# One-column transposes for the last key: ct_fill in a fused perceiver layer

## The chip, the cores and the metric

The kernel runs on one core of a Trainium2 chip. The metric is the device time of one execution in microseconds (us). Engines are called as the profile calls them: PE is TensorE's matmul side and PEld its weight loads, DVE is VectorE, ACT is ScalarE, POOL is GpSimd, SP is SyncE. Everything is fp32 unless it says otherwise.

## The reference

One layer over x (32 batches of 32 tokens, 512 wide) and a context of 257 keys per batch (384 wide). Cut to what matters here:

```python
def _L0_xattn_ref(x, context, g_x, b_x, g_c, b_c, Wq, Wk, Wv, Wo):
    xn = layer_norm(x, g_x, b_x)
    cn = layer_norm(context, g_c, b_c)          # context: (32, 257, 384)
    q = (xn @ Wq) ...; k = (cn @ Wk) ...; v = (cn @ Wv) ...      # 16 heads of 64
    sim = jnp.einsum('bhid,bhjd->bhij', q, k) * scale            # j runs over 257 keys
    attn = jax.nn.softmax(sim, axis=-1)
    out = jnp.einsum('bhij,bhjd->bhid', attn, v)
    return out.transpose(0, 2, 1, 3).reshape(B, N, INNER) @ Wo

x = x + _L0_xattn_ref(_layernorm(x), ctx_768, ...)   # cross attention, 257 keys
x = x + _L0_attn_ref(_layernorm(x), ...)             # self attention, 32 tokens
x = x + _L0_ffn_ref(_layernorm(x), ...)              # 8 experts, the best 2 per token
```

## The kernel before

The work is split into 8 groups of 4 batches (128 tokens). The function `body(g, do_a, do_b, nxt)` writes one round of every engine's instructions in a fixed order: `do_a` is the cross attention of group g, `do_b` the self attention and the routing of group g - 1, and `nxt` prepares group g + 1. Rounds 1 to 6 are a hardware loop; the others are written out. After the last round come the experts (lines 770 to 860). Each engine works through its own list in order and waits on semaphores; what PE does next is therefore exactly what stands next in `body`.

The keys need care: 257 is 128 + 128 + 1. The table `PART = [P, P, 65]` says how many partitions each of the three pieces of a batch's normalised context `ctx` takes. The last key stands on partition 0 of its piece (and copies of it on 32 and 64, which a later split product uses). `ct_fill` turns one 128-column slice c of one batch's context: three transposes on PE, each with `ctx` as the weights and the identity as what streams, write into the bank `TP` at the column offsets `KOFF = [0, 128, 256]`. The last one increments `tp_full`. ACT's `ct_out` (line 1129) then copies `TP[:, 0:KEYS]`, 257 columns, into `cnT` and frees the bank with `tp_free`. `scores` (line 1755) multiplies with `cnT`; the columns of `TP` from 257 on are read by nobody.

There are 3 calls of `ct_fill` per batch, 96 in all. By what stands behind them on PE (in `body`, round by round):

- `scores`, fp32 weights: the calls at b == 0, 3 in each of 8 rounds, 24 in all
- `av`, `av_high` or `av_low`, fp16 weights: the calls at b == 1 and b == 2, 48 in all, and two of the three calls for the next group's first batch, 14 in all; together 62
- another transpose with fp32 weights, `pt_fill` (line 1779) or `setup_fill`: 7 + 1
- another `ct_fill`, which waits for `tp_free`: 2, at the very start

[...]

Of the kernel before, what the change touches and what calls it, by code (L numbers as in the profile page):

```python
# [26 lines left out]
P = 128  # L27
# [17 lines left out]
GB = P // TOK  # L45
# [6 lines left out]
PART = [P, P, 65]  # L52
KOFF = [0, P, 2 * P]
# [41 lines left out]
def perceiver_layer(nc, x, ctx_768, g_x, b_x, g_c, b_c, Wq, Wk, Wv, Wo, W_qkv, W_o,  # L95
                    gate_w, gate_b, w1, b1, w2, b2, ln_g, ln_b, out):
    with ExitStack() as stack:
        def sb(name, shape, dt=F32):
            return stack.enter_context(nc.sbuf_tensor(name, shape, dt))
# [28 lines left out]
        ctx = arena[:, 0:4608].rearrange("p (s k c) -> p s k c", s=GB, k=3)  # L128
# [41 lines left out]
        ident = sb("ident", [P, P])  # L170
# [119 lines left out]
        TP, M, BK = bank[4], [bank[5], bank[6]], bank[7]  # L290
# [1387 lines left out]
        def _(pe):  # L1678
# [80 lines left out]
            def ct_fill(n, bt, b, c):  # L1759
                pe.wait_ge(tp_free, n)  # L1760
                if c == 0:
                    pe.wait_ge(cn_done, bt + 1)
                for k in range(3):
                    last = nc.tensor.transpose(TP[:, KOFF[k]:KOFF[k] + PART[k]], ctx[0:PART[k], b % GB, k, c * P:(c + 1) * P],  # L1764
                                               ident[0:PART[k], 0:PART[k]])
                last.then_inc(tp_full, 1)

            def pt_fill(g, b, k):
# [136 lines left out]
            def body(g, do_a, do_b, nxt):  # L1905
# [4 lines left out]
                if isinstance(g, int) and g == 0:  # L1910
                    pe.wait_ge(wk_in, 16)
                    for n in range(8):
                        setup_fill(n)
                    for c in range(KC):
                        ct_fill(1 + c, 0, 0, c)
                    pe.wait_ge(qkv_in, 16)
                    pe.wait_ge(wos_in, 16)
                    for n in range(8, 16):
                        setup_fill(n)
# [12 lines left out]
                for b in range(GB + 1):  # L1932
                    if do_a and nxt and b == GB:
                        ct_fill(tp(g, ("ct", GB, 0)), GB * g + GB, GB, 0)
                    for h in range(HG):
                        if do_a and b < GB:
                            scores(g, b, h)
                        if do_b and b == 1 and h == 0:
                            v_fill(g - 1)
                        if do_a and b == 0 and h < 3:  # L1940
                            ct_fill(tp(g, ("ct", 1, h)), GB * g + 1, 1, h)
                        if isinstance(g, int) and g == 0 and b == 1 and h in (0, 2):
                            keep_short(16 if h == 0 else 40, BK)
                        if do_a and b >= 1 and h < 3:
                            pt_fill(g, b - 1, h)
# [106 lines left out]
```

## Time and profile before

| | |
|---|---|
| median of 3 runs | 1328.2 us (1325.65 to 1328.8) |
| the profiled execution: its time, its span | 1326.96 us, 1325.3 us |
| mean granted clock of PE | 0.993 |
| PE busy, share of the span | 1277.7 us, 96% |
| PEld, DVE, ACT busy | 72%, 73%, 73% |
| one steady group (round) | 90.2 us |
| the 96 transposes of 65 partitions: records' sum | 21.3 us |

Read it so: a PE record lasts longer than the time that PE gives to it, because records of one engine overlap (they are pipelined). What an instruction costs PE is the distance from its start to the start of the next, here called its slot. The groups' rounds fill the span from about 120 to 740 us with a period of 90.2 us.

### The profile page before, as it was taken

The page shows a single profiled execution, that of the slowest core. Times are in us where ns is not written, and L with a number is a line of the kernel's source. Part 1 is how long each engine was busy: PE and PEld are TensorE (multiplying, and loading weights), DVE is VectorE, ACT ScalarE, POOL GpSimd, SP SyncE. Part 2 cuts the span into 40 slices and gives each one's busy share as a digit, 9 for nine tenths or more (in the row PEclk, how much of TensorE's full clock was granted, in tenths as well). Part 3 has the DMA queues.
Part 4 walks back from the last instruction along what each step waited for, and adds up shares of the span by engine and source line. Part 5 has one row for each costly group of instructions (what it writes and reads, how often), then busy time and mean ns, then how long its engine had stood idle before and what let it go on. Part 6 is the DMA issues. An engine that isn't in the chain of part 4 may idle for free.

```text
span 1325.3 us, 34868 instructions
## 1 busy us (share of the span) xinstructions
PE 1277.7 (96%) x11476; PEld 952.9 (72%) x11477; DVE 971.1 (73%) x2140; ACT 963.9 (73%) x1741; POOL 219.1 (17%) x270
## 2 busy tenths in 40 slices
PE   7999999999999999999999789999999999999997
PEld 7768768677697696786876666777777777777773
DVE  5775878877877878788766757776767676767677
ACT  3577776776777777776877537787888888888784
POOL 1001002012030120030210213121212121111112
PEclk9999999999999999999999889999999999999999
DMA  9527246154363372552732895546262626710104
GB/s 365 191 101 255 90 159 223 63 209 169 99 252 122 110 250 87 182 198 68 255 146 90 317 344 166 222 168 201 95 214 80 228 79 229 277 32 16 32 9 135
DMA packets 69838, 216.36 MB, mean 163 GB/s; under 512 B 5582, under 2 KB 5820, under 8 KB 64652
## 3 DMA queue, kind: packets, MB, share of 16 engines
q1 hardware_dynamic: 63568, 201.71, 42.0%
q0 software_dynamic: 6192, 13.98, 5.1%
q8 instruction: 31, 0.51, 0.1%
q14 instruction: 19, 0.16, 0.0%
q10 hardware_dynamic: 28, 0.01, 0.0%
HBM read 169.46 MB, written 46.22 MB: 163 GB/s over the span
## 4 chain that ended last, share of the span: by engine, by line
PE 67%; DMA 9%; issue 8%; DVE 7%; ACT 4%; POOL 3%; SPq 1%; DVEq 0%; POOLq 0%; ACTq 0%
PE bank L799 7%; PE bank L1755 7%; PE bank L787 6%; PE bank L789 6%; PE bank L801 6%; PE bank L800 6%; PE bank L788 6%; DMA w_halves<-arena 4%; DMA w_halves<-moe_w 3%; PE bank L1804 3%; PE bank L1789 3%; PE bank L1821 3%; PE bank L1792 2%; PE bank L1764 2%; PE bank L1889 2%
## 5 line engine op out<-in xcount | busy, mean ns | idle before, releaser
L787 PE MATMUL bank<-arena,moe_w 128*128 128x128 f16 x1472 | 256.2, 220 | 0.9 <-DVE arena L630 0.9
L789 PE MATMUL bank<-arena,moe_w 128*128 128x128 f16 x1472 | 256.4, 220 | 0.0
L788 PE MATMUL bank<-arena,moe_w 128*128 128x128 f16 x1472 | 255.6, 219 | 0.0
L1755 PE MATMUL bank<-moe_w 128*128 128x257 f32 x768 | 188.6, 383 | 0.0
L787 PEld LDWEIGHTS bank<-arena,moe_w 128*128 (+1 forms) x1472 | 143.8, 98 | 14.9 <-DVE arena L630 1.2
L788 PEld LDWEIGHTS bank<-arena,moe_w 128*128 (+1 forms) x1472 | 144.1, 98 | 10.3
L1755 PEld LDWEIGHTS bank<-moe_w 128*128 128x128 f32 x768 | 137.9, 190 | 17.7
L789 PEld LDWEIGHTS bank<-arena,moe_w 128*128 (+1 forms) x1472 | 143.8, 98 | 1.5 <-issue 0.2
L490 ACT ACTIVATE arena<-bank,now_act 128x128 f32<-128x128 f32 x368 | 136.8, 449 | 7.9 <-PE bank L789 4.5
L506 ACT ACTIVATE wosT<-moe_w,now_act 128x1024 f16 (+1 forms) x90 | 98.5, 1143 | 37.7 <-PE bank L801 37.7
L1147 ACT ACTIVATE moe_w<-bank,cols,ugain 128x512 f32<-128x512 f32 x96 | 74.4, 776 | 59.7 <-PE bank L1805 58.7
L438 POOL DMA_INDIRECT acc_rows<-arena,job_idx x22 | 52.1, 2368 | 396.3 <-DVE arena L671 396.3
L1377 DVE TENSOR_TENSOR moe_w<-bank,moe_w 128x512 f16<-128x512 f32 (+1 forms) x96 | 65.4, 689 | 48.1 <-ACT moe_w L1161 45.8
L647 DVE SCALAR_TENSOR_TENSOR arena<-moe_w,now_v,wosT 128x1024 f16<-128x1024 f16 (+1 forms) x45 | 57.8, 1285 | 52.5 <-ACT wosT L506 50.3
L647 DVE SCALAR_TENSOR_TENSOR kqT<-moe_w,now_v,y 128x1024 f16<-128x1024 f16 (+1 forms) x45 | 57.8, 1285 | 51.3 <-ACT y L506 51.0
L1009 POOL TENSOR_TENSOR crstd<-cmv,half 128x3 f32<-128x3 f32 x32 | 28.7, 898 | 396.1 <-DVE cmv L1334 396.1
L1161 ACT CAST moe_w<-bank 128x512 f16<-128x512 f32 (+1 forms) x96 | 54.3, 585 | 47.2 <-PE bank L1779 46.9
L506 ACT ACTIVATE y<-moe_w,now_act 128x1024 f16 (+1 forms) x45 | 51.7, 1149 | 43.5 <-PE bank L801 43.5
L1789 PE MATMUL bank<-moe_w 128*128 128x512 f16 x192 | 73.0, 380 | 3.7 <-DVE moe_w L1377 1.8
L1792 PE MATMUL bank<-moe_w,arena 128*128 128x512 f16 x192 | 72.6, 378 | 0.0
L1140 ACT ACTIVATE moe_w<-bank,negm 128x257 f32<-128x257 f32 x128 | 59.0, 467 | 15.9 <-DVE negm L1357 15.3
L638 DVE SCALAR_TENSOR_TENSOR arena<-arena,now_h 128x512 f16<-128x512 f32 x92 | 68.7, 746 | 1.6 <-ACT arena L498 1.6
(296 smaller groups left out, 3099.3 us busy)
## 6 DMA issues: line engine op xcount, KB each, us to landing
moe_w<-in_L_ffn_w_dram SPq DMA_DIRECT2D x46, 1024.0 KB, 6.4
moe_w<-w_halves SPq DMA_DIRECT2D x8, 4096.0 KB
moe_w<-in_L_ffn_w_dram SPq DMA_DIRECT2D x8, 4096.0 KB
w_halves<-moe_w SPq DMA_DIRECT2D x48, 512.0 KB, 4.2
arena<-in_ctx_dram SPq DMA_DIRECT2D x32, 384.0 KB
arena<-in_L_ffn_w_dram SPq DMA_DIRECT2D x10, 1024.0 KB, 4.9
blocks<-in_L_ffn_w_dram SPq DMA_DIRECT2D x8, 1024.0 KB, 4.8
w_halves<-arena SPq DMA_DIRECT2D x8, 512.0 KB
```

Of the source, the lines that this page charges most:

```text
L490: last = nc.scalar.activation(h_sb[:, fb % 2, c * P:(c + 1) * P], bank[fb][:, c * P:(c + 1) * P], ACT.Gelu, bias=now_act[:, 4 + 4 * fb + c ...
L506: nc.scalar.activation(v_place(0, j, fb, i), moe_flat[:, bass.ds(slot * 16384 + 8192 + fb * 2048 + i * 1024, 1024)], ACT.Identity, scale=n ...
L647: nc.vector.scalar_tensor_tensor(out=v_place(1, j, fb, i), in0=moe_flat[:, bass.ds(slot * 16384 + 8192 + fb * 2048 + i * 1024, 1024)], sca ...
L787: nc.tensor.matmul(into, high, xT_low[turn][:, k, :], start=(k == 0), stop=False)
L788: nc.tensor.matmul(into, high, xT_high[turn][:, k, :], start=False, stop=False)
L789: last = nc.tensor.matmul(into, low, xT_high[turn][:, k, :], start=False, stop=(k == KD - 1))
L799: nc.tensor.matmul(Y[:, :], hT_low[:, fb % 2, c, :], high, start=(fb == 0 and c == 0), stop=False)
L800: nc.tensor.matmul(Y[:, :], hT_high[:, fb % 2, c, :], high, start=False, stop=False)
L801: last = nc.tensor.matmul(Y[:, :], hT_high[:, fb % 2, c, :], low, start=False, stop=(fb == 3 and c == 3))
L1755: last = nc.tensor.matmul(bank[h][:, 0:KEYS], qkT[:, c, b, h * P:(h + 1) * P], cnT[:, b % 2, c, :], start=(c == 0), stop=(c == KC - 1))
L1789: nc.tensor.matmul(ps[:, :], n_high[:, b % 2, k, columns], pT_high[:, k, :], start=(k == 0), stop=False)
L1792: nc.tensor.matmul(ps[:, :], n_low[:, b, k, columns], pT_high[:, k, :], start=False, stop=False)
```

## The change

In `ct_fill` the third transpose of each call takes 1 partition and 1 column (`n_rows = 1`), where it took 65 and 65. It writes column 256 of `TP` alone. The first two transposes, the semaphores and all other engines' instructions are as they were; `PART` itself is unchanged, so the normalisation and the split products still handle 65 partitions.

```diff
@@ ct_fill
                 for k in range(3):
-                    last = nc.tensor.transpose(TP[:, KOFF[k]:KOFF[k] + PART[k]], ctx[0:PART[k], b % GB, k, c * P:(c + 1) * P],
-                                               ident[0:PART[k], 0:PART[k]])
+                    n_rows = P if k < 2 else 1
+                    last = nc.tensor.transpose(TP[:, KOFF[k]:KOFF[k] + n_rows], ctx[0:n_rows, b % GB, k, c * P:(c + 1) * P],
+                                               ident[0:n_rows, 0:n_rows])
                 last.then_inc(tp_full, 1)
```

[...]

PE's list at b == 1, where a call of `ct_fill` stands between two fp16 products of `av` (a row is: line, operation, output<-inputs, output's partitions x columns, how many in a row), before:

```order
L1805 MATMUL bank<-moe_w 128x512
L1764 MATMUL bank<-ident,arena 128x128 x2
L1764 MATMUL bank<-ident,arena 128x65
L1789 MATMUL bank<-moe_w 128x512
L1792 MATMUL bank<-moe_w,arena 128x512
```

and now (the line numbers are one higher):

```order
L1806 MATMUL bank<-moe_w 128x512
L1765 MATMUL bank<-ident,arena 128x128 x2
L1765 MATMUL bank<-ident,arena 128x1
L1790 MATMUL bank<-moe_w 128x512
L1793 MATMUL bank<-moe_w,arena 128x512
```

Nothing moved; one row is narrower. PE's list at b == 0, where the calls stand between `scores` (line 1755), before:

```order
L1755 MATMUL bank<-moe_w 128x257 x3
L1764 MATMUL bank<-ident,arena 128x128 x2
L1764 MATMUL bank<-ident,arena 128x65
L1755 MATMUL bank<-moe_w 128x257 x3
L1764 MATMUL bank<-ident,arena 128x128 x2
```

and now:

```order
L1755 MATMUL bank<-moe_w 128x257 x3
L1765 MATMUL bank<-ident,arena 128x128 x2
L1765 MATMUL bank<-ident,arena 128x1
L1755 MATMUL bank<-moe_w 128x257 x3
L1765 MATMUL bank<-ident,arena 128x128 x2
```

Again only the third transpose differs, and the order is the same on every engine.

## Rows read from the trace of the kernel before

**Rows 1.** The page: busy time, granted clock, the chain's shares.
```profile
PE 1277.7 (96%) x11476; PEld 952.9 (72%) x11477; DVE 971.1 (73%) x2140; ACT 963.9 (73%) x1741; POOL 219.1 (17%) x270
...
PEclk9999999999999999999999889999999999999999
...
PE 67%; DMA 9%; issue 8%; DVE 7%; ACT 4%; POOL 3%; SPq 1%; DVEq 0%; POOLq 0%; ACTq 0%
```
**Rows 2.** Windows: stretch, length, PE, PEld, DVE, ACT, POOL busy, clock, DMA share.
```profile
290.00:380.20 90.20, 88.66 (x682) 67.78 (x682) 71.94 (x191) 66.04 (x117) 14.51 (x18) 1.00 0.46 160
...
790.00:1325.00 535.00, 522.69 (x5570) 370.51 (x5566) 375.87 (x560) 421.38 (x780) 99.62 (x104) 0.99 0.42 139
```
**Rows 3.** Groups by line and shape: weights, what streams, count, busy us, mean ns.
```profile
L1764 PE MATMUL bank<-ident,arena 128*128 128x128 f32 x192 | 39.7, 288 | 4.8 <-ACT moe_w L1129 2.1 <-DVE moe_w L1377 2.0
...
L1889 PE MATMUL bank<-wosT,kqT 128*128 128x512 f32 x64 | 28.9, 593 | 0.5 <-ACT kqT L1165 0.5
L1764 PE MATMUL bank<-ident,arena 65*128 65x65 f32 x96 | 21.3, 222 | 0.0
...
L1994 PE MATMUL bank<-ident,arena 8*128 8x8 f32 x16 | 1.1, 201 | 0.0
...
L1870 PE MATMUL bank<-arena,kqT 128*32 128x128 f32 x32 | 1.1, 276 | 0.0
```
**Rows 4.** Timeline of PE: one call of ct_fill; start us, duration us, what.
```profile
158.71 0.38 PE L1805 MATMUL bank<-moe_w 65*128 65x512 f16 x1
158.93 0.44 PE L1764 MATMUL bank<-ident,arena 128*128 128x128 f32 x3
159.21 0.38 PE L1789 MATMUL bank<-moe_w 128*128 128x512 f16 x1
```
**Rows 5.** Timeline of PE: from 128x128 tiles to 128x64 tiles.
```profile
180.69 3.60 PE L1889 MATMUL bank<-wosT,kqT 128*128 128x512 f32 x8
184.22 5.73 PE L1821 MATMUL bank<-moe_w 128*64 128x128 f32 x96
```
**Rows 6.** Timeline of PE: into 128x32 tiles and out of them.
```profile
145.15 0.38 PE L1805 MATMUL bank<-moe_w 65*128 65x512 f16 x1
145.47 1.08 PE L1870 MATMUL bank<-arena,kqT 128*32 128x128 f32 x32
146.48 0.50 PE L1764 MATMUL bank<-ident,arena 128*128 128x128 f32 x3
```
**Rows 7.** Timeline of PE and PEld: into 32x128 tiles and out, last round.
```profile
767.71 1.45 PE L1889 MATMUL bank<-wosT,kqT 128*128 128x512 f32 x3
769.09 0.39 PE L1974 MATMUL bank<-ident,most_rows 16*128 16x16 f32 x2
...
769.56 1.13 PE L1994 MATMUL bank<-ident,arena 8*128 8x8 f32 x16
770.62 0.61 PE L1687 MATMUL bank<-ident 128*128 128x256 f16 x4
...
770.62 0.44 PEld L1687 LDWEIGHTS bank<-ident 128*128 128x128 f16 x5
```
**Rows 8.** Timeline of PE: scores behind line 1739, then behind ct_fill.
```profile
37.09 1.57 PE L1755 MATMUL bank<-moe_w 128*128 128x257 f32 x6
...
38.78 1.52 PE L1755 MATMUL bank<-moe_w 128*128 128x257 f32 x6
```
**Rows 9.** Timeline of DVE, ACT and PEld: third ct_fill of a steady round.
```profile
310.29 0.55 DVE L1308 TENSOR_SCALAR arena<-x_all,mv,rstd 128x512 f32 x1 [0.68 <-POOL rstd L1004]
...
311.21 0.48 ACT L1140 ACTIVATE moe_w<-bank,negm 128x257 f32<-128x257 f32 x1 [0.96 <-DVE negm L1357]
...
312.70 0.31 PEld L1764 LDWEIGHTS bank<-ident,arena 128*128 128x128 f32 x3 [0.46 <-ACT moe_w L1129]
```
**Rows 10.** Waits of PE in the steady round: us, times, longest.
```profile
PE bank L1764 <- DVE moe_w L1377: 0.3, 2, 0.2
PE bank L1833 <- ACT moe_w L1134: 0.3, 1, 0.3
```

## Prediction

> **What bounds the kernel now.** I read the page first. PE is busy for 96% of the span and holds 67% of the chain, while DVE and ACT stand at 73% [rows 1]. [...] The waits say the same: PE's two largest in the round are 0.3 us each, and all five rows of that answer together make 1.3 us [rows 10]. So during the rounds PE's own list sets the pace, and whatever a call of `ct_fill` costs more or less is paid almost in full, 96 times. The experts behind (535 us, [rows 2]) start when the rounds are over and hold no `ct_fill`; they shift as a block.
>
> **What the third transpose costs today.** Its record lasts 222 ns [rows 3], but that is not its price. In one call the three transposes start at 158.93 and `av`'s first product at 159.21 [rows 4]: 0.28 us for three slots. The two wide ones take 0.109 us each (three records last 0.44 us together, and the last of them 0.222, so two slots are 0.22), which leaves 0.06 us for the third. The whole that could be saved is thus 96 x 0.06 = 5.8 us, not the 21.3 us of the records' sum.
>
> **What it would cost if nothing but the width changed.** [...] The nearest row is line 1994: 16 transposes of 8 columns start 62 ns apart (1.13 us for 16, the last lasting 0.20, so 15 slots in 0.93) [rows 3, 7]. With an fp32 operation behind it the slot of a one-column transpose therefore stays at 0.06. Behind it stands fp16 in 62 calls; there the bounds are 0 and 0.06 us saved, and I would take half, 0.03 us, 2 us in all. [...]
>
> [...] The trace has passages between tiles, and each shows the same gap:
> - Into 128x64: eight records of line 1889 last 3.60 us, the last 0.593 [rows 3, 5], so their slots are 3.01 / 7 = 0.43, and the last starts at 183.70. Line 1821 starts at 184.22, 0.52 later: 0.09 more than a slot.
> - Into 128x32: line 1805 has 0.32 us before line 1870 [rows 6], and 0.22 us before line 1764, which has its own tile [rows 4]: 0.10 more.
> [...]
> - Out of 128x32: the last record of line 1870 starts at 145.47 + 1.08 - 0.276 = 146.27, line 1764 at 146.48 [rows 3, 6]: 0.20 for 128 fp32 columns that take 0.11, so again 0.09 to 0.10.
> [...]
>
> [...]
>
> The second part of the price is the weights. After a passage the load is no longer hidden: three transposes of line 1764 last 0.50 us behind line 1870 and 0.44 where their weights came early [rows 4, 6], 0.06 for fp32 transpose weights; `scores` takes 1.57 us behind line 1739's 64x128 tile and 1.52 behind `ct_fill` [rows 8], 0.05 more. For fp16 weights (line 1687, 1789) I take 0.01; no row above separates it, and 0 to 0.03 are its bounds.
>
> **One call, from the second transpose's start to the next operation's start.** Before: 0.11 + 0.06 = 0.17. After: 0.11, drain 0.09, the third's own weights 0.06, its one column practically 0, drain 0.10: 0.36. That is +0.19, and with the next operation's exposed weights +0.20 before fp16 and +0.24 before fp32. The lower bound takes the own load as hidden and the way out as line 1994 showed it: 0.09 + (0.13 - 0.06) = 0.16. The upper bound is +0.26 everywhere.
>
> **The sum.** 62 calls x 0.20 = 12.4; 24 + 8 calls before fp32 x 0.24 = 7.7; the two at the start, where PE waits for ACT anyway and only the bank's filling comes later (0.09 + 0.06), 0.3. Together 20.4 us.
>
> **What waits give back.** Where PE stands still today for something that does not depend on the calls just before, the delay fills the hole. One such place is clear. In each round the third call at b == 0 waits (0.46 us by the loader's row, 312.70) for ACT's `ct_out`, which is queued behind an exp that waited 0.96 us for DVE, which had waited for POOL's rstd [rows 9]. None of these comes after the first two calls. Line 1755 ahead lets PE start every 0.22 us; the wide first transpose came about 0.22 late and with its weights exposed (0.06): 0.28 us a round, 2.2 us in 8. The calls behind `av` wait a little for ACT too; I give them another 0.8 us. That makes 3 us absorbed. Bounds: nothing, and all 1.3 us of a round's waits [rows 10], 10 us in 8 rounds. Most of these waits follow PE's own `pt_fill` through ACT and DVE and would only move, so I stay near the lower. ACT gets `tp_full` 0.15 us later in each call, which ACT, busy 66 of 90 us, can take; and if DVE or ACT fell behind through it the next to be late would be `scores`' row maximum.
>
> 20.4 - 3.0 = +17.4 us. The profiled execution took 1326.96 us (span 1325.3), so 1344.4; the median shown is 1.2 us above it. I predict **1345 us**.
>
> **Rivals.**
> - *The forecast*: two drains a call, 1345 us (1338 to 1351 as its own range). [...] Chance 0.78.
> - [...] Chance 0.04, of which 0.03 lie within 0.3%. [...]
> - *Half price*: the way in or the way out overlaps with the transposes around it, so a call costs 0.10 to 0.12: 96 x 0.11 - 2 = +8.5, 1336 us. For it: no row shows a single instruction in a foreign tile; each passage above has several on either side. Chance 0.10.
> - *More than the sum*: `tp_full`'s delay also lengthens the chain through ACT and DVE, or a lone instruction pays 0.26 with nothing absorbed: +25, 1353 us. Against it: ACT and DVE have 18 us to spare per round [rows 2]. Chance 0.08.
>
> **How the numbers follow.** A measurement of this kernel can tell about 0.3%, 4 us, from no change. Faster by more 0.01; within 0.03; slower 0.96. The range of 8 in 10 leaves out the not-slower case, half of the half-price case, and the far end above: 1337 to 1351.
>
> **What would show it.** In the profile after, line 1765's record of one partition should start 0.20 us after the second transpose (0.11 before), and the operation behind it 0.15 to 0.17 us later (0.06 before). Its weight load should start with it and not ahead, and the next load should start only with the next operation. The steady round should last 92.2 to 92.6 us where it lasted 90.2, the experts' stretch should stay at 535 us, and the third call at b == 0 should no longer wait. The clock should stay at 1.00 in the rounds. I am wrong if that narrow record starts 0.11 after the second transpose, or if the round grows by less than 1.5 us with the gaps as forecast: then waits took more than I allowed.

## The result

The changed kernel takes 1341.2 us (median of 6 runs, 1336.8 to 1343.3), the kernel before 1327.4 us in the same comparison (6 runs): ratio 1.0099, interval 1.0084 to 1.0114. It is slower by 13.8 us or 1.0%. Forecast were 1345 us, a range of 1337 to 1351, and slower.

The page of the changed kernel, to be read against [rows 1]: PE is busier (1297.5 us against 1277.7), its weight loads take 8 us more, and the other engines are as they were. PE's share of the chain is 83% where it was 67%; a second profile of the same kernel has 73%, so nothing below rests on it.

```profile
PE 1297.5 (97%) x11476; PEld 961.1 (72%) x11477; DVE 971.7 (72%) x2140; ACT 963.6 (72%) x1741; POOL 218.0 (16%) x270
...
PE 83%; DVE 5%; ACT 5%; DMA 3%; issue 2%; POOL 1%; DVEq 0%; POOLq 0%; ACTq 0%; SPq 0%
```

Its groups by line and shape, to be read against [rows 3]: the narrow transpose's record is 4 ns shorter (218 against 222). By that row nothing has changed; the loss stands only in the distances between starts, and in the loader's idle time, 16.1 us or 0.17 us for each of the 96, with nothing that it waited for.

```profile
L1765 PE MATMUL bank<-ident,arena 1*128 1x1 f32 x96 | 21.0, 218 | 0.0
...
L1765 PEld LDWEIGHTS bank<-ident,arena 1*128 1x128 f32 x96 | 12.9, 134 | 16.1 <-issue 16.1
```

Timeline of PE and PEld in the changed kernel, one call before an fp16 product (start us, duration us, what), to be read against [rows 4]:

```profile
162.94 0.53 PE L1765 MATMUL bank<-ident,arena 128*128 128x128 f32 x3
...
163.25 0.14 PEld L1765 LDWEIGHTS bank<-ident,arena 1*128 1x128 f32 x1 [0.17 <-issue]
163.40 0.10 PEld L1790 LDWEIGHTS bank<-moe_w 128*128 128x128 f16 x1
163.41 0.39 PE L1790 MATMUL bank<-moe_w 128*128 128x512 f16 x1
```

From the first transpose to the product it is 0.47 us, where it was 0.28: unrounded, 0.18 more. Three records last 0.53, the last 0.218, so the third starts at 163.25, 0.20 us after the second (two wide slots of 0.11 would have put it at 163.16), and the product comes 0.15 after it (0.06 before). Each of the two weight loads starts only when its operation does (163.25, and 163.40 for the product at 163.41). These are the two gaps that the forecast calls drains.

What the traces show is the weights' partitions x columns and the starts. No view prints an array tile, and none shows the array being emptied; where the prediction and the titles of [rows 5, 6, 7] speak of tiles and drains, they are my reading of the gaps. In [rows 7] the weights are 16*128 and 8*128. Below, a passage is a change of the weights' partitions x columns after which PE's next start is 0.07 to 0.10 us later than its slots account for. Not every change is one: from line 1805's 65*128 weights to line 1764's 128*128 it is 0.22 us [rows 4], as between two products of 128*128 (141.96 to 142.18, lines 1789 and 1792 of the kernel before).

The windows, round by round (stretch, length, busy times, clock, DMA). First a steady round of the changed kernel, then rounds 0 to 3 of a second profile of it (the run e10 below), in all four of which the clock was 1.00:

```profile
389.26:480.74 91.48, 90.56 (x682) 68.36 (x683) 71.92 (x191) 65.93 (x117) 14.27 (x18) 1.00 0.45 157
```
```profile
11.53:110.02 98.49, 93.38 (x747) 73.72 (x746) 64.52 (x173) 58.94 (x114) 7.29 (x9) 1.00 0.59 212
110.02:203.52 93.50, 90.50 (x684) 68.29 (x682) 69.81 (x176) 68.99 (x120) 9.86 (x13) 1.00 0.44 152
203.52:295.18 91.66, 90.60 (x682) 68.36 (x683) 72.01 (x191) 65.89 (x117) 14.42 (x18) 1.00 0.44 157
295.18:386.75 91.57, 90.60 (x683) 68.37 (x683) 71.97 (x191) 65.93 (x117) 14.37 (x18) 1.00 0.45 158
```

and the same rounds of the kernel before, cut at the same places in its program:

```profile
11.59:108.18 96.59, 91.15 (x747) 73.25 (x746) 64.14 (x172) 58.69 (x114) 7.29 (x9) 1.00 0.59 216
108.18:199.79 91.61, 88.57 (x683) 67.70 (x682) 69.78 (x176) 68.92 (x120) 9.85 (x13) 1.00 0.46 157
199.79:290.05 90.26, 88.66 (x682) 67.78 (x683) 71.97 (x191) 65.83 (x117) 14.41 (x18) 1.00 0.45 159
290.05:380.24 90.19, 88.66 (x682) 67.78 (x683) 71.93 (x191) 66.04 (x117) 14.51 (x18) 1.00 0.46 160
```

So rounds 0 and 1 grew by 1.9 us each and the steady ones by 1.4. The forecast had 2.0 to 2.4 for a steady round. Twelve calls cost clearly more than the round grew, and the experiments look for the difference. One more sign of the forecast did not hold in the first profile: its clock was not at 1.00 in all the rounds, but 0.83 at 120 to 130 us (see e10).

### The profile page after: what moved, and what is told of

Its sections match the earlier page's. It is cut to its first block, busy times and chain, and to the rows that moved or that the text cites. A ratio compares the mean times of both kernels' runs of the same rounds, so it can differ in the third digit from the quotient of the medians.

```text
span 1340.3 us, 34868 instructions
## 1 busy us (share of the span) xinstructions
PE 1297.5 (97%) x11476; PEld 961.1 (72%) x11477; DVE 971.7 (72%) x2140; ACT 963.6 (72%) x1741; POOL 218.0 (16%) x270
## 4 chain that ended last, share of the span: by engine, by line
PE 83%; DVE 5%; ACT 5%; DMA 3%; issue 2%; POOL 1%; DVEq 0%; POOLq 0%; ACTq 0%; SPq 0%
PE bank L1755 9%; PE bank L799 6%; PE bank L787 6%; PE bank L789 6%; PE bank L801 6%; PE bank L800 6%; PE bank L788 6%; PE bank L1718 4%; PE bank L1834 4%; PE bank L1790 3%; PE bank L1739 3%; PE bank L1805 3%; PE bank L1822 3%; PE bank L1765 3%; PE bank L1793 3%
```

## The experiments

All times are medians. e2, e3, e4 and e7 ran on one chip, beside a kernel before at 1326.4 us; e5, e6, e8 and e10 on another, beside one at 1327.5. "Call" is the distance from a call's first transpose to the operation behind it, at b == 0; it is 0.28 us in the kernel before and 0.46 in the changed one. All of them replace the loop in `ct_fill`; the diffs are against the changed kernel, written with this helper:

```python
def turn(k, rows):
    return nc.tensor.transpose(TP[:, KOFF[k]:KOFF[k] + rows], ctx[0:rows, b % GB, k, c * P:(c + 1) * P],
                               ident[0:rows, 0:rows])
```

**e2: 33 partitions instead of 1.**

```diff
-                    last = turn(k, P if k < 2 else 1)
+                    last = turn(k, P if k < 2 else 33)
```

> [...] Theory (the passage between tiles costs, whatever the tile): the third starts 0.20 us after the second and the next operation about 0.17 us after it (0.15 with one column, and 33 fp32 columns stream 0.03 longer), so about 2 us above the changed kernel, 1343 us. [...]

Measured: 1343.0 us, ratio 1.0123 (1.0104 to 1.0142). Timeline of PE, one call:

```profile
407.25 0.56 PE L1764 MATMUL bank<-ident,arena 128*128 128x128 f32 x3
407.74 1.57 PE L1755 MATMUL bank<-moe_w 128*128 128x257 f32 x6
```

The call takes 0.49 us, 0.03 more than with one column. The third starts at 407.56, 0.20 us after the second, as in the changed kernel, and `scores` 0.18 after it, where it is 0.15 with one column. So it is no matter of one partition: 33 have the same two gaps, but for the 32 further columns, and the slots of 0.11 and 0.06 did not come back. The weights of line 1739, 64*128, have the gap on the way in too: 124.91 to 125.12 in the kernel before, 0.10 over line 1855's slot of 0.11. Beside weights of 128*128, those of 1, 8, 16, 33 and 64 partitions have a gap and those of 65 have none (e3); by what rule, no run shows.

**e4: the one-partition transpose twice in a row.**

```diff
                 turn(0, P)
                 turn(1, P)
+                turn(2, 1)
                 last = turn(2, 1)
```

> [...] Theory (price per passage): the second one starts 0.06 us after the first, its weights in the same tile, so 0.06 us a call more, 1345 to 1347 us. Rival (price per narrow instruction): again 0.20 and 0.15, so 0.2 to 0.3 us a call more, 1362 to 1368 us.

Measured: 1345.5 us, ratio 1.0143 (1.0127 to 1.0158). The call:

```profile
411.60 0.59 PE L1764 MATMUL bank<-ident,arena 128*128 128x128 f32 x4
412.12 1.57 PE L1755 MATMUL bank<-moe_w 128*128 128x257 f32 x6
```

0.52 us, 0.06 more than with one. Inside the call the narrow ones start at 411.91 and 412.00:

```profile
412.00 0.20 PE L1764 MATMUL bank<-ident,arena 1*128 1x1 f32 x1
412.12 0.48 PE L1755 MATMUL bank<-moe_w 128*128 128x257 f32 x1
```

So the second starts 0.085 us after the first, not the 0.06 of the expectation, and the next operation 0.125 after the second, where it is 0.147 after a single one. The two together make the 0.06. The price of a passage is not paid again; it belongs to the change from wide weights to narrow ones and back, and not to the narrow instruction. One column more costs, net, the 0.06 us that line 1994's eight did.

**e5: four passages instead of two.**

```diff
                 turn(0, P)
+                turn(2, 1)
                 turn(1, P)
                 last = turn(2, 1)
```

> Order of a call: wide, one-partition, wide, one-partition (the first one-partition transpose is a repeat of the last). Four passages where the changed kernel has two, and as many narrow transposes as in the kernel that did it twice in a row. Theory (each passage 0.09 us plus the weights that it exposes): 0.09 + 0.15 + 0.06 = 0.30 us a call over the changed kernel, and as the waits of the round are used up already nearly all of it shows: the steady round takes 94.8 to 95.1 us, the run 1366 to 1370 us. Rival (the price was that of a narrow transpose or of the end of a call): 0.06 us a call as with twice in a row, 1346 us.

Measured: 1367.0 us, ratio 1.0298 (1.0281 to 1.0316). The call, and the steady round:

```profile
423.33 0.83 PE L1764 MATMUL bank<-ident,arena 128*128 128x128 f32 x4
424.09 1.57 PE L1755 MATMUL bank<-moe_w 128*128 128x257 f32 x6
```
```profile
404.18:498.97 94.79, 93.80 (x694) 70.29 (x695) 71.99 (x191) 66.38 (x117) 15.82 (x18) 1.00 0.44 153
```

The same four instructions as in e4, two of them in another order: 0.76 us a call against 0.52. In the whole it is 39.5 us over the kernel before on its chip, where e4 is 19.1 over the one on its own: 20.4 more. This is the strongest of the runs, since the instructions are the same and only their order, and with it the number of passages, differs. Over the changed kernel a call costs 0.30 us more, 3.6 us in a round of twelve, and 3.25 of them show (94.79 against 91.54 in e10).

**e6: two passages, but with wide transposes on both sides.**

```diff
                 turn(0, P)
-                turn(1, P)
-                last = turn(2, 1)
+                turn(2, 1)
+                last = turn(1, P)
```

> Order of a call: wide, one-partition, wide; the wide one increments the semaphore. Two passages as in the changed kernel, but what stands behind the narrow one always has fp32 transpose weights, whose load is exposed. Theory: slots 0.20, 0.15 and 0.165 us, so 0.05 us more in the 62 calls that fp16 products follow, 2 to 3 us over the changed kernel, 1343 to 1345 us. Rival (the delay of the semaphore to ACT was part of the price): the same as the changed kernel or less, 1339 to 1341 us.

Measured: 1341.6 us, ratio 1.0110 (1.0094 to 1.0126). That lies between the theory's 1343 to 1345 and the rival's 1339 to 1341. It is 3.4 us over e10 on the same chip, but e10's six runs spread over 6 us, and e6's steady round (91.67 us) is only 0.13 over e10's (91.54), about 1 us in eight rounds. The time does not decide; the starts do. The call:

```profile
407.30 0.68 PE L1764 MATMUL bank<-ident,arena 128*128 128x128 f32 x3
407.82 1.47 PE L1755 MATMUL bank<-moe_w 128*128 128x257 f32 x6
```

At b == 0 the call is longer (0.52), but the six records of `scores` behind it last 1.47 instead of 1.57 us: their weights came early, behind a wide transpose (the load starts at 407.65, 0.17 us ahead of the product; in the changed kernel both start together, at 408.81). From one such call to the next it is 1.82 us here, 1.87 in the changed kernel and 1.64 before: the exposed load has moved into the call, and 0.04 of the price is saved. Before fp16 products the call is 0.05 to 0.06 longer, as the theory had it.

**e3: as much delay without a passage.** The third transpose keeps 65 partitions; two wide ones ahead of it write columns that nobody reads.

```diff
                 turn(0, P)
                 turn(1, P)
+                for _ in range(2):
+                    nc.tensor.transpose(TP[:, 3 * P:4 * P], ctx[0:P, b % GB, 1, c * P:(c + 1) * P], ident[:, :])
-                last = turn(2, 1)
+                last = turn(2, PART[2])
```

> The 65-partition transpose as before the change, and two more wide transposes ahead of it into columns of the bank that nobody reads: 0.22 us more per call with no tile passage. Theory (of what a call costs more, waits elsewhere in the round give back about 1.1 us a round, and PE's clock falls in the changed kernel because it streams less): the steady round grows by 2.6 - 1.1 = 1.5 us, to 91.7 us, the clock stays at 1.00 up to 200 us, the run takes about 1340 us. Rival (waits give back 0.4 us a round as forecast, and the passages have some gain of their own): the round grows by 2.2 us, 1345 us.

Measured: 1338.7 us, ratio 1.0098 (1.0084 to 1.0113). The steady round:

```profile
387.92:479.57 91.65, 90.73 (x707) 70.65 (x707) 71.99 (x191) 65.86 (x117) 16.36 (x18) 1.00 0.45 158
```

Here the 65-partition transpose starts at 407.50, 0.11 us after the one ahead, and `scores` at 407.56: no gap on either side. Twelve calls x 0.22 = 2.6 us more of PE work make the round 1.5 us longer (91.65 against 90.15 to 90.19). About 1.1 us comes back, whatever the delay consists of. So the missing part of the changed kernel's price is no cheapness of the gaps; it is given back by waits. Its expectation on the clock was only half right: at 120 to 200 us it was 1.00, but this profile has a low stretch earlier (0.79 at 8 to 16 us), ahead of the first `ct_fill`.

**e7: no third transpose.** The last key's column is whatever the bank held, so this computes something else; it is a bound.

```diff
                 turn(0, P)
-                turn(1, P)
-                last = turn(2, 1)
+                last = turn(1, P)
```

> The third transpose is left out altogether, so the last key's column of the keys is whatever the bank held; this bounds what any form of it can be worth. Theory (0.06 us a call, and waits for ACT and DVE grow back by a part of it): 5.8 us gross, 2 to 4 us net, 1323 to 1325 us. Rival (hidden anyway): 1327 us.

Measured: 1323.1 us, ratio 0.9968 (0.9954 to 0.9983). The steady round takes 89.84 us, 0.3 less. With the transpose gone the third call at b == 0 waits again:

```profile
380.60:470.44 89.84, 87.99 (x670) 66.82 (x671) 71.87 (x191) 66.07 (x117) 14.84 (x18) 1.00 0.46 161
```
```profile
403.23 0.44 PE L1764 MATMUL bank<-ident,arena 128*128 128x128 f32 x2 [0.29 <-ACT moe_w L1129]
```

The medians differ by 3.3 us; by the interval of the ratio it is 2.3 to 6.1. So no form of the third transpose can be worth more than about that, under half a per cent, unless it also shortens those waits.

**e10: the changed kernel again**, with 5 rounds.

> The changed kernel once more, beside the others on one chip: 1336 to 1343 us as before. Its profile shows whether the two stretches of low clock (24 to 32 and 120 to 128 us) belong to the change or come and go; if they come and go, a profile without them takes 1337 us, 10 us over the kernel before.

Measured: 1338.2 us (1336.6 to 1342.6), ratio 1.0085 (1.0069 to 1.0102), +10.8 us. The profiled execution, without the two stretches, took 1339.0 us, where 1337 was expected. Windows of PE's clock in its profile, and in the first one:

```profile
20.00:30.00 10.00, 7.95 (x76) 7.05 (x76) 5.91 (x12) 5.62 (x11) 0.00 (x0) 1.00 1.04 397
120.00:130.00 10.00, 8.31 (x99) 7.93 (x100) 6.70 (x8) 6.79 (x12) 3.87 (x4) 1.00 0.50 197
```
```profile
20.00:30.00 10.00, 7.94 (x53) 7.05 (x53) 4.46 (x8) 5.02 (x10) 0.00 (x0) 0.83 1.04 398
120.00:130.00 10.00, 8.21 (x74) 7.54 (x72) 5.53 (x6) 6.07 (x9) 3.86 (x4) 0.83 0.42 169
```

The low stretches come and go with one and the same program. What the first costs is in the timelines, 32 transposes of line 1698: 5.38 us in the first profile, 3.71 in this one.

```profile
23.71 5.38 PE L1698 MATMUL bank<-ident,moe_w 128*128 128x128 f32 x32
```
```profile
24.48 3.71 PE L1698 MATMUL bank<-ident,moe_w 128*128 128x128 f32 x32
```

**e8: the first batch's three calls stay wide.**

```diff
-                    last = turn(k, P if k < 2 else 1)
+                    last = turn(k, P if k < 2 else (PART[2] if isinstance(bt, int) and bt == 0 else 1))
```

> The changed kernel, but the first batch's three calls, at the very start, keep the 65-partition transpose. Theory (the low clock at 24 to 32 us in the changed kernel's profile comes by chance of how idle PE is there, and the three calls matter little): 0.5 us less than the changed kernel, 1339 to 1341 us, low clock there now and then still. Rival (the narrow transposes at the start bring the low clock about): the clock is 1.00 there and 2 us are saved, 1338 to 1339 us.

Measured: 1338.4 us (1335.2 to 1340.9), ratio 1.0080 (1.0065 to 1.0094), no difference from e10 that shows. In its profile the clock is 1.00 at 20 to 30 us, but 0.83 at 8 to 18 us, before any narrow transpose, and 0.83 at 120 to 130 us. The time and the clock at 20 to 30 us are those of the rival, yet e10 has the same time and the same clock there with the narrow transposes in, so they don't speak for it. The stretch at 8 to 18 us needs no narrow transpose. Those near 24 and 123 us are another matter: of the seven profiles with narrow transposes ahead of 200 us (the changed kernel, e2, e4, e5, e6, e8, e10) five have one or both of them; the kernel before, e3 and e7 have neither. Ten profiles don't settle whether the change makes them more frequent.

## Why the prediction was right, and where it was off

**Two gaps a call: right.** The trace before had them at several changes of the weights: the three that the prediction lists, and two at narrow weights [rows 7]. Line 1974, with 16*128, starts 0.52 us after the last record of line 1889 (768.57 to 769.09), 0.09 over its slot of 0.43, and line 1687 starts 0.13 after the last of line 1994 (770.49 to 770.62), together with its weight load. Each of the 96 new pairs has a single instruction between its two gaps, and they are as long. The third starts 0.20 us after the second, as forecast; the next operation 0.15 after the third (forecast 0.15 to 0.17). e5 against e4 shows the cause: same instructions, two more passages, 20.4 us. The forecast's terms of 0.09 and 0.10 were put down to a drain when PE changes its array tile. No run shows a drain or a tile; shown is the gap, 0.09 on the way in and 0.13 from a start with ready weights to the next operation on the way out.

**The own weights: 0.02, not 0.06.** e4 separates them. From the narrow transpose to the operation behind it is 0.147 us when it is alone, and 0.125 when it comes second of the two, with its weights ready; line 1994's way out had taken the same 0.13 [rows 7]. So the exposed load adds 0.02 and not 0.06. The way out by itself takes 0.13 and not 0.10, and the two errors nearly cancel: 0.15 stands where the forecast added up 0.16. That the sum of a call was right is in this part luck. Why so little of the load shows, no run tells.

**The next operation's weights: right.** Before fp16 the starts show under 0.01 us. `scores` behind a call lasts 1.57 us where it lasted 1.52 [rows 8], and 1.47 where a wide transpose stands between (e6).

The gross price so becomes 0.18 us before fp16 weights and 0.23 to 0.24 before fp32: 62 x 0.18 + 32 x 0.235 = 18.7 us, where the forecast had 20.4.

**What waits give back: the step that was mis-sized.** I gave 3 us for the whole, which is less than 0.4 us a round. A round's twelve calls cost 8 x 0.18 + 4 x 0.235 = 2.4 us, and a steady round grew by 1.4, so 1.0 us came back in each. The prediction named this case (the round growing by less than 1.5 us with the gaps as forecast), and it happened: by its own sign the price of a call was right and the term for the waits wrong. Following the starts of the same instructions through a steady round of the kernel before and one of e10 shows where PE makes up for the delay, and it is at four places.

The first is the one that I had named, and its size was right: 0.28 us at the third call at b == 0. In the changed kernel's timeline that call stands 1.87 us after the second, as the second does after the first, with no wait.

```profile
408.35 0.53 PE L1765 MATMUL bank<-ident,arena 128*128 128x128 f32 x3
...
410.22 0.53 PE L1765 MATMUL bank<-ident,arena 128*128 128x128 f32 x3
...
412.09 0.53 PE L1765 MATMUL bank<-ident,arena 128*128 128x128 f32 x3
```

The second is at the calls behind `av`: 0.10 us at the middle one of each batch's three at b == 1 and b == 2, 0.20 a round, where I had given 0.1. The other two I had left out, taking them for waits that would only move. Behind `pt_fill` the first product waited for ACT, and no longer does; 0.24 us come back there. Timeline of the kernel before, then of e10:

```profile
354.68 0.39 PE L1789 MATMUL bank<-moe_w 128*128 128x512 f16 x1 [0.21 <-ACT moe_w L1161]
```
```profile
361.18 0.39 PE L1790 MATMUL bank<-moe_w 128*128 128x512 f16 x1
```

And at the end of the round PE waited for ACT's copy [rows 10, line 1833]. Timeline of the kernel before:

```profile
371.17 0.63 PE L1848 MATMUL bank<-ident,arena 128*128 128x128 f32 x4
372.11 1.32 PE L1833 MATMUL bank<-moe_w 128*128 128x256 f32 x5 [0.32 <-ACT moe_w L1134]
```

and of the changed kernel:

```profile
472.00 0.60 PE L1849 MATMUL bank<-ident,arena 128*128 128x128 f32 x4
472.63 2.18 PE L1834 MATMUL bank<-moe_w 128*128 128x256 f32 x9
```

0.94 us from the one to the other became 0.63, and with the transposes just ahead 0.39 us come back. ACT had run behind PE in this stretch, with the experts' weights to scale (its copy started at 371.40, after line 1188); a slower PE let it catch up. The waits of the changed kernel's steady round say the same: of the five rows three are left, and the two for ACT are gone.

```profile
PE bank L1765 <- DVE moe_w L1377: 0.3, 2, 0.2
PE bank L1780 <- DVE moe_w L1377: 0.3, 1, 0.3
PE bank L1790 <- DVE moe_w L1377: 0.2, 1, 0.2
```

Together the four places give 0.28 + 0.20 + 0.24 + 0.39 = 1.1 us, of which the two that I had put at nothing are more than half. My upper bound, all of the round's listed waits, was 1.3 us; e2 (1.1), e3 (1.1) and e4 (1.2) come near it, and e5 (1.4 of 6.0 us) passes it. It was no true bound: the list holds idle time between records, and the 0.28 us at b == 0 and the 0.20 behind `av` stand under the records that overlap. I had chosen near the wrong end of a range that held the value.

**The sum.** 18.7 - 8 = +10.7 us would come from 1.0 us in each of eight rounds, and e10 measured +10.8. But that agreement is in part luck. By the windows of e10 and of the kernel before, rounds 0 and 1 grew by 1.9 us each, the five steady ones by 1.4, the last by 2.1 (with nine calls, 1.8 us), and the experts took 0.7 less. That adds up to 12.1 us, which is what these two profiled executions differ by. Round 0 holds the three calls of the start besides its twelve, and in round 1 one wait grew: PE's for ACT's line 1104 went from 1.3 to 1.8 us. The last round and the experts, before and in e10:

```profile
650.50:783.25 132.75, 119.35 (x933) 90.58 (x932) 91.01 (x251) 76.16 (x125) 24.76 (x31) 0.95 0.60 217
783.25:1325.30 542.05, 528.56 (x5652) 375.98 (x5652) 381.19 (x577) 427.11 (x790) 100.21 (x105) 0.99 0.43 141
```
```profile
661.16:796.05 134.89, 123.02 (x934) 92.66 (x932) 91.09 (x251) 76.04 (x125) 24.19 (x31) 0.94 0.59 215
796.05:1337.40 541.35, 528.24 (x5652) 375.94 (x5652) 381.08 (x577) 427.49 (x790) 99.50 (x105) 1.00 0.43 142
```

The first comparison measured +13.8; forecast was +17.4. Its profile holds two stretches of low clock ahead of 200 us that e10's doesn't, and the one that can be read from line 1698 cost 1.7 us. The runs' mean clocks point the same way: the four of the twelve runs of the changed kernel with 0.988 took 1341.9 to 1343.3 us (three of them in the first comparison, one in e10), the eight with 0.991 to 0.994 took 1336.6 to 1340.5. So the 3 us between the two comparisons go with the clock; that it alone makes them is not shown.

**The rivals.** That the change only narrows the slot, the case with chance 0.04, is refuted by the start times: 0.20 us where 0.11 would stand. "Half price", 1336 us, is nearer to e10's 1338.2 than the forecast is, for the wrong reason: the calls cost nearly full price, and the waits gave a third of it or more back. "More than the sum" did not happen. ACT's copy of line 1129 stands on the changed kernel's chain once a round, but it starts 0.68 us after ACT's own line 1147, as it did before, and does not wait for the later `tp_full`.

**The experts** took 542.05 and 541.35 us (cut at their first transpose) and only shifted.

## What to carry to other kernels

On a TensorE that sets the pace, read a matmul's cost from the distance between starts, not from its record: here the record got 4 ns shorter and the call 0.18 us longer. Before narrowing an operation, look in the trace for what a change from its neighbours' weights to such narrow ones does to the starts; the idle rows and columns were cheaper here (0.06 us from the third transpose of 65*128 between 128*128 weights, against 0.24 with 1*128: a gap of 0.09 and 0.15 to the next start). And when a small delay repeats in a loop, count how much of each round PE waits for engines that run behind it: about that much, here 1 of 2.4 us, can come back, and a wait that hides under overlapping records counts too.

## What the runs showed of the hardware that was not expected

- The way in costs the same for weights of 1, 16 and 33 partitions, single or several in a row, 0.09 us (the changed kernel, line 1974 [rows 7], e2). From the narrow one's start to the next operation it is 0.13 us when its weights were ready (e4), 0.15 when they were not, and 0.18 with 33 columns (e2).
- The granted clock fell to 0.50 for about 3 us in some executions and not in others (windows of 1 us at 24 to 27 us in the first profile of the changed kernel): of the changed kernel at 20 to 30 and 120 to 130 us, in e3 and e8 also at 8 to 18 us. PE had been waiting for ACT at 20 to 24 us in both profiles of the changed kernel, 0.66 us a time, and the clock fell in one of them.
